# Attention results moved by transfers within SBUF, denominators on eight rows, gate by exponential, a first lead of 20 slots

## The chip, the cores and the metric

The kernel runs on one core of one Trainium2 chip. The metric is the device time of the whole kernel in microseconds, the median of several runs. All matrix work is TensorE's (PE), and DVE, ACT (ScalarE) and POOL (GpSimd) are the engines beside it; SP only issues transfers and waits.

## The reference

One layer of a transformer on x of 4 x 1024 x 128 in f32, cut to what matters:

```
a   = layernorm(layernorm(x)) * ln_g + ln_b           # the inner one is the block's, the outer the attention's
q, k, v = split(a @ w_qkv + b_qkv)                     # 16 heads of 8 dimensions
p   = softmax(q k^T / sqrt(8) + relative_bias)         # 1024 x 1024 for each of 4 x 16 heads
x   = x + layernorm((p v) @ w_out + b_out)
h   = layernorm(x)
s   = sigmoid(h @ gate^T);  sfc = s + e_bias           # 64 experts in 8 groups
eight experts of the four best groups by sfc; weights s / sum(s) * 2.5; capacity 128 per expert
y   = sum of weight * w2(silu(w1 h) * (w3 h))  +  a shared expert of the same form
out = x + layernorm(y)
```

## The kernel before

The 4096 tokens are 8 chunks of 512 (4 tiles of 128). The kernel has four parts, one behind the other.

*Projection (project_tokens).* For each chunk the tokens are normalised, transposed and multiplied by w_qkv. q and k are cut into three bf16 pieces each and stored to DRAM as q_image and k_image; v gets its bias by an addition on DVE (add_v, L291) and is stored as v_columns with a column of ones behind each head's eight, nine in all. DVE fills the fixed rows of the stacks at the very start (L296). The relative bias is a product of sines too: its query and key rows stand in bias_q_image and bias_k_image, and load_bias_side (L141) loads them into the stacks of four groups of four heads, group 0's on SP's queue here, those of groups 1 to 3 on ACT's queue at the start of the next part: 54 transfers.

*Attention and routing (attend_and_route).* There are 32 units: a batch, one half of its queries (512) and a group of four heads. Each engine has its own instruction stream, written out in steps; 32 steps make a unit. In a step TensorE makes a transposed score of 128 keys by 512 queries (scores_t, L1219) in one of three banks (st_bank), and ACT takes its exponential (L1141) into probs. The order in which users take the three banks is a list (ring_places): each place waits until the place three before it is free. In every second step TensorE makes one slot of row scores (row_scores, L1206) in one of two double banks, and DVE takes its maximum (row_max, L692); 16 slots make a unit, and they run LEAD = 26 slots ahead of the steps. When the maxima of a unit are complete, POOL splits the negative maximum in two bf16 pieces (split_shift), TensorE transposes it (turn_shift, L1242, at step J_MTURN = 18 of the unit before), ACT copies it (shift_copy, L1059), and SP puts it into the query stack with four transfers (put_shift, L636). The first step of the unit waits for them.

Every four steps TensorE multiplies the probabilities with the values (times_values, L1228): four heads side by side in four column tiles, 9 columns each, into one bank (pv_bank). The products stand after steps PV_AFTER = (9, 13, 16, 20, 24, 27, 31, 35). In the next unit ACT copies the bank to unit_out (out_copy, L1066, step 4), TensorE transposes it in four pieces (turn_out, L1237, step 8), and ACT copies the result to att (rows_copy, L1075): rows are tokens then, and the ninth column of each head is its denominator.

When four units have given 512 tokens of 16 heads, the chunk is routed while the next four units run: DVE takes reciprocals of 128x64 denominators (L719), POOL multiplies (normalise, L913), TensorE transposes (turn_att), ACT copies (copy_att), TensorE multiplies with w_o, and so on through two layer norms, the transposition of the result (L1264), the gate's logits, and ACT's Sigmoid (gate_scores, L1111). Sigmoid and Exp are in different activation tables. The selection of the experts goes to and fro between DVE and POOL. RING_AT, NORM_Y, RECIP and their like say in which unit of four and at which step each piece stands; NORMALISE, BIASED and their like do the same for POOL, in eighths of a unit. POOL writes each chunk's rows to the experts' table with 32 indirect transfers (scatter, L1002), one in each eighth of a unit; those of the last chunks run behind the last unit.

*SP's queue.* Before: loads of groups 1 to 3, the first shift, 12 constants, and then in each unit the next batch's loads of one group (13 transfers, 12 units have them), the next shift, and clearing of the tables.

*Experts (run_experts) and the last layer norm (finish)* follow. They are not touched.

Of the kernel before, what the change touches and what calls it, by code (L numbers as in the profile page):

```python
# [18 lines left out]
ALU = mybir.AluOpType  # L19
# [3 lines left out]
P = 128  # L23
# [11 lines left out]

VW = HD + 1
# [64 lines left out]
class Stacks:  # L101
# [3 lines left out]
    def __init__(self, ctx, nc):  # L105
# [4 lines left out]
        self.values = [sb(f"values{g}", [P, TILES_T, HG, VW]) for g in range(GROUPS)]  # L110
# [6 lines left out]
        self.vst = [sb(f"vst{a}", [P, PER, H, VW]) for a in range(2)]  # L117
# [15 lines left out]
def load_values(engine, stacks, v_columns, b, g):  # L133
    engine.dma_start(stacks.values[g][:].rearrange("p k h c -> p k (h c)"),
                     v_columns[:, b * TILES_T:(b + 1) * TILES_T, HG * VW * g:HG * VW * (g + 1)]).then_inc(stacks.loaded[g], 16)

# [4 lines left out]
def load_bias_side(engine, stacks, bias_q_image, bias_k_image, g, side):  # L141
    mine = slice(SIDE_HEADS * side, SIDE_HEADS * (side + 1))
    heads = slice(HG * g + SIDE_HEADS * side, HG * g + SIDE_HEADS * (side + 1))
    for r, places in Q_PLACED(side, bias=True):
        engine.dma_start(stacks.q[g][r:r + 2 * HD, :, mine, :].rearrange("r c h i -> r c (h i)"),
                         bias_q_image[:, places, :, heads, :].rearrange("c u e h i -> (u e) c (h i)")).then_inc(stacks.bias_rows_in[g], 16)
    for r, places in K_PLACED(side, bias=True):
        for c in range(2):
            engine.dma_start(stacks.k[g][r:r + 2 * HD, c, mine, :],
                             bias_k_image[c, places].rearrange("u e (o i) -> (u e) o i", o=1).to_broadcast([2 * HD, SIDE_HEADS, CHUNK])).then_inc(stacks.bias_rows_in[g], 16)  # L150


LOAD_BIAS = 16 * 9 * SIDES


def project_tokens(nc, x, ln_g, ln_b, w_qkv, b_qkv, w_rel_rows, q_table, k_table, ident_in, ident,
# [3 lines left out]
    with ExitStack() as ctx:  # L160
# [12 lines left out]
        bv = sb("bv", [P, DIM])  # L173
# [11 lines left out]
        half_made, ones_made, scaled_b = sem("half_made"), sem("ones_made"), sem("scaled_b")  # L185
# [8 lines left out]
        CONSTS, BIAS_CONSTS = 8 * 16, 3 * 16  # L194
# [3 lines left out]
        def _(sp):  # L198
# [4 lines left out]
            for dst, src in (  # L203
# [4 lines left out]
                (bv[:], b_qkv[2 * DIM:3 * DIM].rearrange("(o d) -> o d", o=1).to_broadcast([P, DIM])),  # L208
# [12 lines left out]
            for c in range(CHUNKS):  # L221
# [8 lines left out]
                sp.dma_start(v_columns[:, c * PER:(c + 1) * PER, :], vst[a][:].rearrange("p j h c -> p j (h c)")).then_inc(v_stored[a], 16)  # L230
# [8 lines left out]
                if c in (1, 2):  # L239
                    load_bias_side(sp, stacks, bias_q_image, bias_k_image, 0, c - 1)  # L240
# [11 lines left out]
        def _(dve):  # L252
# [33 lines left out]
            def add_v(c):  # L286
                a = c % 2
# [1415 lines left out]
```

## Time and the profile before

| | |
|---|---|
| median of 3 runs | 1190.63 us (1190.5 to 1190.64) |
| profiled execution | 1190.24 us, of which the span is 1188.4 us |
| mean granted clock | 0.882 |
| PE busy | 895.0 us (75%) |
| DVE busy | 782.7 us (66%) |
| ACT busy | 718.9 us (60%) |
| POOL busy | 579.1 us (49%) |
| first transposed score | 111.6 us |
| last copy out of the value bank | 903.9 us |
| first expert's rows loaded from the table | 1011.8 us |

The shares of busy time are means over stages with different limits, so they are read by stage. An engine's idle time is given with what ended it. A matmul's length in the timeline contains its way through the array; the distance between two starts is what it holds the engine. Some matmul records are missing.

### The profile page before, as it was taken

The numbers are of one execution on the slowest core, as the hardware profiler recorded it, in microseconds if no ns is written. First come the engines' busy times: TensorE is split into PE (matmuls) and PEld (weight loads), VectorE is DVE, ScalarE is ACT, GpSimd is POOL, SyncE is SP. The second block draws the span as 40 slices with busy tenths as digits, with TensorE's granted clock in tenths as the row PEclk, the third lists the DMA queues.
The fourth block names the chain that finished last, engine by engine and source line by source line (L and its number), as shares of the span: only waits on it lengthen the run. The fifth ranks groups of instructions, "written<-read, shape, count | busy, mean of one in ns | idle before, by whom it ended". The sixth has DMA issues, their size and how long they took to land. (4 is left out here: it accounts for less than half of the span.)

```text
span 1188.4 us, 16269 instructions
## 1 busy us (share of the span) xinstructions
PE 895.0 (75%) x5166; PEld 292.5 (25%) x5248; DVE 782.7 (66%) x1222; ACT 718.9 (60%) x1452; POOL 579.1 (49%) x724
## 2 busy tenths in 40 slices
PE   4545999999999999998999999999886450655400
PEld 2310222222222222222222222222222330443300
DVE  7977888779788888887987887897730320111107
ACT  4521777787787778778778877877885110322204
POOL 5621000112455454544644554463566775478847
PEclk9865999999999999999999999999998675656655
DMA  4798110122410022210001111000000010767546
GB/s 101 232 238 119 34 54 28 48 68 62 103 34 26 25 55 54 70 35 3 3 3 35 34 41 27 3 3 2 2 2 3 28 37 11 186 125 136 101 95 210
DMA packets 109292, 73.59 MB, mean 62 GB/s; under 512 B 39711, under 2 KB 94747, under 8 KB 109206
## 3 DMA queue, kind: packets, MB, share of 16 engines
q1 hardware_dynamic: 84470, 63.01, 19.7%
q0 software_dynamic: 21504, 6.79, 4.8%
q10 hardware_dynamic: 3232, 2.73, 1.6%
q8 instruction: 42, 0.69, 0.2%
q14 instruction: 44, 0.36, 0.1%
HBM read 39.99 MB, written 54.95 MB: 80 GB/s over the span
## 5 line engine op out<-in xcount | busy, mean ns | idle before, releaser
L692 DVE TENSOR_REDUCE half_max<-s_pair 128x2 f32<-128x1024 f32 x512 | 602.9, 1217 | 138.7 <-PE s_pair L1206 134.1
L1141 ACT ACTIVATE probs<-st_bank 128x512 f32<-128x512 f32 x1024 | 554.8, 602 | 173.8 <-PE st_bank L1219 147.5
L1002 POOL DMA_INDIRECT table<-rows,keys_i x256 | 255.5, 998 | 258.9 <-PE pv_bank L1228 120.1
L1219 PE MATMUL st_bank<-q_stack,k_stack 98*128 98x512 bf16 (+1 forms) x942 | 320.8, 387 | 35.2 <-ACT probs L1141 25.5
L1228 PE MATMUL pv_bank<-probs,values 128*9 128x512 f32 x2048 | 267.7, 595 | 1.9 <-issue 0.2
L1206 PE MATMUL s_pair<-k_stack,q_stack 64*128 64x512 bf16 x1024 | 205.7, 399 | 21.6 <-DVE half_max L692 19.8
L1219 PEld LDWEIGHTS st_bank<-q_stack,k_stack 98*128 98x128 bf16 (+1 forms) x1024 | 81.6, 97 | 252.1 <-ACT probs L1141 150.3
L1415 POOL DMA_INDIRECT sums<-out,ids x64 | 99.0, 1547 | 41.5 <-ACT out L1470 18.7
L1206 PEld LDWEIGHTS s_pair<-k_stack,q_stack 64*128 64x128 bf16 x1024 | 49.2, 93 | 275.6 <-issue 160.4
L1429 DVE CAST ids<-xe 128x4 uint32<-128x4 f32 x16 | 2.7, 168 | 131.6 <-DMA sums<-out,ids 84.8
L1506 PE MATMUL psY<-down_w,h 64*128 64x128 f32 x128 | 18.4, 434 | 46.4 <-DVE h L1442 46.4
L898 POOL CAST shift<-minus_max 128x16 bf16<-128x16 f32 x32 | 6.8, 212 | 94.9 <-DVE minus_max L699 93.9
L1470 ACT ACTIVATE out<-psY,w_cur 128x128 f32<-128x128 f32 x64 | 18.3, 368 | 55.8 <-PE psY L1506 55.2
L1483 PE MATMUL psX<-const_ident,xe 128*128 128x128 f32 x64 | 16.5, 407 | 45.8 <-DMA xe<-table 45.8
L1228 PEld LDWEIGHTS pv_bank<-probs,values 128*9 128x9 f32 x2048 | 30.3, 88 | 67.5 <-issue 39.9
L1603 ACT ACTIVATE whole<-whole,lessE,rstdE 128x128 f32<-128x128 f32 x32 | 13.2, 482 | 43.4 <-POOL lessE L1596 43.4
L1454 ACT COPY xeT<-psX 128x512 f32<-128x512 f32 x16 | 9.4, 585 | 40.2 <-PE psX L1483 33.6
L1495 PE MATMUL psH<-xeT,up_w 128*64 128x128 f32 x256 | 30.3, 413 | 2.3 <-issue 1.7
L1059 ACT CAST shiftT<-st_bank 32x128 bf16<-32x128 f32 x32 | 7.7, 240 | 32.7 <-issue 32.7
L1237 PE MATMUL st_bank<-const_ident,unit_out 128*128 128x128 f32 x128 | 20.1, 280 | 9.1 <-ACT probs L1141 8.2
L1506 PEld LDWEIGHTS psY<-down_w,h 64*128 64x128 f32 x128 | 13.9, 298 | 52.2 <-DVE h L1442 52.2
L1495 PEld LDWEIGHTS psH<-xeT,up_w 128*64 128x64 f32 x256 | 24.0, 214 | 5.9 <-issue 4.7
(181 smaller groups left out, 803.4 us busy)
## 6 DMA issues: line engine op xcount, KB each, us to landing
table<-blank SPq DMA_DIRECT2D x8, 772.0 KB, 4.8
xe<-table SPq DMA_DIRECT2D x16, 386.0 KB, 5.1
q_stack<-q_image SPq DMA_DIRECT2D x96, 64.0 KB
k_stack<-k_image SPq DMA_DIRECT2D x96, 64.0 KB
s<-sums SPq DMA_DIRECT2D x24, 256.0 KB, 6.1
k_image<-k_piece SPq DMA_DIRECT2D x16, 256.0 KB, 2.9
table<-rows,keys_i POOLq DMA_INDIRECT x256
sums<-zeros SPq DMA_DIRECT2D x16, 256.0 KB
```

The costliest lines, as they stand in the source:

```text
L692: V.tensor_reduce(half_max[n % 2][:, h:HG:SIDE_HEADS, tile, half], s_pair[slot % S_SLOTS][:].rearrange("p (s k) -> p s k", s=SIDES), AX.X, ...
L1002: pool.indirect_dma_start(out=table, out_offset=bass.IndirectOffsetOnAxis(ap=keys_i[c % 2][:, pick:pick + 1], axis=0), in_=rows[c % 2][:, ...
L1141: A.activation(probs[:, s % P_SLOTS, :], st_bank[at % ST_BANKS][:], ACT.Exp).then_inc(bank_free, 1)
L1206: mm = M(s_pair[slot % S_SLOTS][:, side * CHUNK:(side + 1) * CHUNK], q_stack[g][own, half, head, tile * P:(tile + 1) * P], k_stack[g][own, ...
L1219: M(bank(at)[:], k_stack[g][own, tile // PER, h, tile % PER * P:(tile % PER + 1) * P], q_stack[g][own, half, h, :], start=True, stop=True) ...
L1228: mm = M(pv_bank[PART * h:PART * h + VW, :], values[n % GROUPS][:, tile, h, :], probs[:, (s + h) % P_SLOTS, :], start=(tile == 0), stop=(t ...
L1237: mm = nc.tensor.transpose(to[:, t * P:(t + 1) * P], unit_out[:, t * P:(t + 1) * P], ident[:])
L1415: pool.indirect_dma_start(out=sums[n % SUMS], out_offset=bass.IndirectOffsetOnAxis(ap=ids[a][:, q:q + 1], axis=0), in_=out[a][:, q, :], in ...
L1470: A.activation(out[r % DEEP][:, q, :], psY[q % 2][:, q // 2 * P:(q // 2 + 1) * P], ACT.Copy, scale=w_cur[r % DEEP][:, q:q + 1]).then_inc(o ...
L1483: mm = nc.tensor.transpose(psX[a][:, q * P:(q + 1) * P], xe[r % DEEP][:, q, 0:DIM], ident[:])
L1495: mm = M(psH[a][half:half + F, m * P:(m + 1) * P], up_w[a][:, (which * Q + q) * F:(which * Q + q + 1) * F], xeT[a][:, q * P:(q + 1) * P], ...
L1506: mm = M(psY[q % 2][:, m * P:(m + 1) * P], h[a][half:half + F, m * P:(m + 1) * P], down_w[a][half:half + F, m * DIM:(m + 1) * DIM], start= ...
```

## The change

1. *Values.* The values are stored with 8 columns a head, without bias and without ones, sorted by dimension and then head. ACT copies them (copy_v). One tensor, values, holds for each tile 32 value columns and 32 ones that are filled once. A head's product takes every fourth column of the 64: 8 values and 8 ones, 16 columns for 9, so that its denominator comes out on eight rows.
2. *Moves.* Eight transfers on SP for each unit (move_out) put each head's eight result rows and eight denominator rows from unit_out to the partitions of its dimensions in sums_t and denominators: the chunk is then already transposed. turn_out, rows_copy, turn_att and copy_att are gone. The reciprocal is over 128x512 elements, POOL multiplies, and the result is projected.
3. *Bias of the values.* Since the probabilities sum to one, it is multiplied with w_o once (value_bias) and added to the output's bias (output_bias) in unit 2.
4. *Gate.* ACT takes exp(-x), POOL adds one, DVE takes the reciprocal of 128x256.
5. *Start.* SP loads group 1, then puts the first shift, then loads groups 2 and 3; the constants come behind the shift of unit 1. ACT loads the query rows of the bias from DRAM and copies the key rows from group 0's stack, 30 transfers for 54. 20 slots run ahead at first, and one more is added every eight steps up to 26. POOL's set-up follows the second shift.
6. *Places.* The value products stand after steps 7, 11, 15, 19, 23, 27, 31 and 35; most places of the routing move by 2 to 6 steps, and the scatters by an eighth of a unit.

```diff
-        self.values = [sb(f"values{g}", [P, TILES_T, HG, VW]) for g in range(GROUPS)]
+        self.values = sb("values", [P, GROUPS, TILES_T, 2, HD * HG])
...
+def copy_bias_keys(engine, stacks, g, side):
+    for r, rows in ((MAIN_AT[side] + MAIN_ROWS, MAIN_ROWS), (REST_AT[side] + REST_ROWS, REST_ROWS)):
+        engine.dma_start(side_of(stacks.k[g], r, rows, side), side_of(stacks.k[0], r, rows, side)).then_inc(stacks.bias_rows_in[g], 16)
...
-            def add_v(c):
...
-                V.tensor_tensor(vst[a][:, :, :, 0:HD], psV[a][:].rearrange("p (j h d) -> p j h d", j=PER, h=H),
-                                bv[:].rearrange("p (o h d) -> p o h d", o=1, h=H).to_broadcast([P, PER, H, HD]), ALU.add).then_inc(v_done, 1)
...
+            V.memset(stacks.values[:, :, :, 1, :].rearrange("p g k c -> p (g k) c"), 1.0).then_inc(stacks.gaps_done, 1)
...
+            def copy_v(c):
...
+                for j in range(PER):
+                    ins = A.copy(vst[a][:, :, j, :].rearrange("p g (d h) -> p g h d", h=HG), psV[a][:, j * P:(j + 1) * P].rearrange("p (g h d) -> p g h d", g=GROUPS, h=HG))
...
-PV_AFTER = (9, 13, 16, 20, 24, 27, 31, 35)
-J_UOUT, J_OTURN, J_MTURN = 4, 8, 18
+PV_AFTER = (7, 11, 15, 19, 23, 27, 31, 35)
+J_UOUT, J_BO = 4, 10
+BO_UNIT = 2
...
-RING_AT = {"att": (0, 17), "y": (0, 22), "xf": (1, 25), "logits": (1, 30), "ranks": (3, 2)}
-NORM_Y, NORM_XF = (1, 2), (1, 18)
-RECIP, STATS_Y, STATS_X1 = (0, 12), (0, 26), (1, 10)
-TOP1, COUNT, SECOND, GSUM, GRANK, BEST, MARK, WEIGHTS, KEYS = (2, 6), (2, 8), (2, 12), (2, 14), (2, 20), (2, 24), (2, 26), (3, 2), (3, 10)
+RING_AT = {"y": (0, 26), "xf": (1, 28), "logits": (1, 31), "ranks": (3, 4)}
+NORM_Y, NORM_XF = (1, 4), (1, 22)
+RECIP, STATS_Y, STATS_X1 = (0, 18), (0, 30), (1, 14)
+GATE, TOP1, COUNT, SECOND, GSUM, GRANK, BEST, MARK, WEIGHTS, KEYS = (2, 6), (2, 10), (2, 12), (2, 16), (2, 18), (2, 24), (2, 28), (2, 30), (3, 6), (3, 14)
...
-NORMALISE, OUT_NORM, RESIDUAL, RES_NORM = (0, 3), (0, 7), (1, 2), (1, 4)
-BIASED, TOPS, ORDER, KEEP, CHOOSE, SLOTS_AT = (2, 1), (2, 2), (2, 4), (2, 5), (2, 7), (3, 1)
-SPLIT, SCATTER = 3, 3 * TILES_T + 3
+NORMALISE, OUT_NORM, RESIDUAL, RES_NORM = (0, 5), (0, 7), (1, 2), (1, 5)
+GATE_ONE, BIASED, TOPS, ORDER, KEEP, CHOOSE, SLOTS_AT = (2, 0), (2, 2), (2, 3), (2, 5), (2, 6), (3, 0), (3, 2)
+SPLIT, SCATTER = 3, 3 * TILES_T + 4
...
+def MTURN(n):
+    return 22 if n == 0 else 18
...
+def issued(step):
+    return min(ALL_UNITS * SLOTS, step // 2 + 1 + FIRST_LEAD + min(LEAD - FIRST_LEAD, step // 8))
...
+            def move_out(n):
+                c, g = n // GROUPS, n % GROUPS
+                sp.wait_ge(unit_out_done, n + 1)
+                if c >= 1 and g == 0:
+                    sp.wait_ge(normed_done, c)
+                for h in range(HG):
+                    to = slice((HG * g + h) * HD, (HG * g + h + 1) * HD)
+                    for v, dst in enumerate((sums_t, denominators)):
+                        sp.dma_start(dst[to, :], unit_out[PART * h + v * HD:PART * h + (v + 1) * HD, :]).then_inc(unit_moved, 16)
...
-                V.reciprocal(recip[:], att[c % 2][:, :, :, HD]).then_inc(recip_done, 1)
+                dve.wait_ge(unit_moved, MOVED * GROUPS * (c + 1))
+                V.reciprocal(denominators[:], denominators[:]).then_inc(recip_done, 1)
+            def gate_scores(c):
+                dve.wait_ge(plus_one_done, c + 1)
+                V.reciprocal(scores[:], scores[:]).then_inc(gate_done, 1)
...
+                G.tensor_tensor(att[:], sums_t[:], denominators[:], ALU.mult).then_inc(normed_done, 1)
...
+            act.wait_ge(bias_rows_in[0], LOAD_BIAS[0])
             for g in range(1, GROUPS):
                 for side in range(SIDES):
-                    load_bias_side(act, stacks, bias_q_image, bias_k_image, g, side)
+                    load_bias_queries(act, stacks, bias_q_image, g, side)
+                    copy_bias_keys(act, stacks, g, side)
...
-                    act.wait_ge(bank_ready, after(place["out", n - 1]))
+                    act.wait_ge(unit_moved, MOVED * n)
                 A.copy(unit_out[:], pv_bank[:]).then_inc(unit_out_done, 1)
...
-                A.activation(scores[:].rearrange("p t e -> p (t e)"), st_bank[at % ST_BANKS][:, 0:PER * E], ACT.Sigmoid).then_inc(bank_free, 1)
+                A.activation(scores[:].rearrange("p t e -> p (t e)"), st_bank[at % ST_BANKS][:, 0:PER * E], ACT.Exp, scale=-1.0).then_inc(bank_free, 1)
...
-                    mm = M(pv_bank[PART * h:PART * h + VW, :], values[n % GROUPS][:, tile, h, :],
+                    mm = M(pv_bank[PART * h:PART * h + 2 * HD, :],
+                           values[:, n % GROUPS, tile].rearrange("p u c -> p (u c)")[:, h:2 * HD * HG:HG],
                            probs[:, (s + h) % P_SLOTS, :], start=(tile == 0), stop=(tile == TILES_T - 1),
```

## Rows read from the trace of the kernel before

**Rows 1.** View of stages, two stretches: busy us, (instructions), clock, DMA share, GB/s.

```profile
200.00:300.00 100.00, 93.51 (x561) 25.20 (x569) 83.72 (x115) 78.26 (x155) 18.79 (x38) 1.00 0.22 60
...
900.00:1000.00 100.00, 42.40 (x163) 24.48 (x159) 20.32 (x63) 19.69 (x37) 72.98 (x87) 0.69 0.08 23
```

**Rows 2.** Timeline of a regular stretch, all engines: start us, length us, what, [idle before].

```profile
180.03 1.05 PE L1228 MATMUL pv_bank<-probs,values 128*9 128x512 f32 x8
...
181.01 0.39 PE L1206 MATMUL s_pair<-k_stack,q_stack 64*128 64x512 bf16 x2
...
181.33 0.60 PE L1219 MATMUL st_bank<-q_stack,k_stack 98*128 98x512 bf16 x2
...
181.44 2.36 DVE L692 TENSOR_REDUCE half_max<-s_pair 128x2 f32<-128x1024 f32 x2 [0.34 <-PE s_pair L1206]
...
181.75 1.57 ACT L1141 ACTIVATE probs<-st_bank 128x512 f32<-128x512 f32 x3 [0.64 <-PE st_bank L1219]
...
182.73 1.05 PE L1228 MATMUL pv_bank<-probs,values 128*9 128x512 f32 x8
```

**Rows 3.** Timeline of PE, where other work comes in.

```profile
163.34 0.63 PE L1237 MATMUL st_bank<-const_ident,unit_out 128*128 128x128 f32 x4 [0.19 <-ACT probs L1141]
...
171.24 0.23 PE L1242 MATMUL st_bank<-ident,shift 128*32 128x128 bf16 x1 [0.25 <-issue]
...
258.46 0.39 PE L1219 MATMUL st_bank<-q_stack,k_stack 128*128 128x512 bf16 x1 [1.53 <-ACT probs L1141]
...
258.78 0.62 PE L1228 MATMUL pv_bank<-probs,values 128*9 128x512 f32 x4
```

**Rows 4.** Timeline of ACT, copies out of the value bank, one per unit.

```profile
184.95 0.58 ACT L1066 COPY unit_out<-pv_bank 128x512 f32<-128x512 f32 x1
...
208.27 0.58 ACT L1066 COPY unit_out<-pv_bank 128x512 f32<-128x512 f32 x1
...
233.44 0.59 ACT L1066 COPY unit_out<-pv_bank 128x512 f32<-128x512 f32 x1
...
261.00 0.58 ACT L1066 COPY unit_out<-pv_bank 128x512 f32<-128x512 f32 x1
...
308.52 0.58 ACT L1066 COPY unit_out<-pv_bank 128x512 f32<-128x512 f32 x1
```

**Rows 5.** Timeline of the start of the attention, several engines.

```profile
94.57 0.29 PE L1242 MATMUL st_bank<-ident,shift 128*32 128x128 bf16 x1 [2.43 <-POOL shift L900]
...
101.61 0.25 ACT L1059 CAST shiftT<-st_bank 32x128 bf16<-32x128 f32 x1 [32.74 <-issue]
...
101.89 2.87 SPq L636 DMA_DIRECT2D q_stack<-shiftT  x4
...
111.62 1.03 PE L1219 MATMUL st_bank<-q_stack,k_stack 98*128 98x512 bf16 x2 [5.16 <-DMA q_stack<-shiftT]
```

**Rows 6.** View of DMA issues: count, KB each, median us to landing.

```profile
k_stack<-bias_k_image SPq DMA_DIRECT2D x12, 32.0 KB, 2.0
```

**Rows 7.** Groups of instructions: count, busy us, mean ns, idle before.

```profile
L1228 PEld LDWEIGHTS pv_bank<-probs,values 128*9 128x9 f32 x2048 | 30.3, 88 | 67.5 <-issue 39.9 <-ACT probs L1141 17.4 <-ACT shiftT L1059 5.7
...
L719 DVE RECIPROCAL recip<-att 128x64 f32<-128x64 f32 x8 | 4.4, 544 | 16.0 <-ACT att L1075 16.0
...
L785 DVE RECIPROCAL wrec<-wsum 128x4 f32<-128x4 f32 x8 | 1.4, 178 | 0.3
...
L1111 ACT ACT_TABLE_LOAD x7 | 9.0, 1283 | 0.1
```

**Rows 8.** Timeline of SP, one load's issue.

```profile
237.91 0.43 SPq L134 DMA_DIRECT2D values<-v_columns  x1
```

**Rows 9.** Timeline of DVE and POOL behind the last unit.

```profile
905.49 0.55 DVE L719 RECIPROCAL recip<-att 128x64 f32<-128x64 f32 x1 [15.99 <-ACT att L1075]
...
933.41 0.97 POOL L1002 DMA_INDIRECT table<-rows,keys_i  x1 [0.30 <-issue]
...
934.40 0.74 POOL L949 TENSOR_TENSOR sfc<-scores,const_e_bias 128x256 f32<-128x256 f32 x1
```

More of the change, by code:

```diff
@@ L345, in _ @@
             inverse(0)
-            for a in range(2):
-                G.memset(vst[a][:, :, :, HD:VW], 1.0).then_inc(ones_made, 1)
             inverse(1)
@@ L502, in ring_places @@
                 order.append(("step", n * STEPS + j))
-            if j == J_OTURN and 1 <= n <= ALL_UNITS:
-                order.append(("out", n - 1))
-            if j == J_MTURN and n < ALL_UNITS - 1:
+            if n < ALL_UNITS - 1 and j == MTURN(n):
                 order.append(("shift", n + 1))
+            if (n, j) == (BO_UNIT, J_BO):
+                order.append(("bo", 0))
             if n >= GROUPS:
@@ L664, in _ @@
                 if n == 0:
+                    for dst, src in later:
+                        sp.dma_start(dst, src, allow_slow_non_contiguous=True).then_inc(later_in, 16)
                     sp.wait_ge(zeros_done, 1)
@@ L807, in shared_h @@
                 V.tensor_tensor(s_h[c % 2], s_pair[c % 2][:, CHUNK:2 * CHUNK], s_h[c % 2], ALU.mult).then_inc(s_h_done, 1)
[L809 removed]
+            for slot in range(FIRST_LEAD):
                 row_max(slot)
@@ L1021, in _ @@
                         residual_norm(c)
+                    elif now and at == GATE_ONE:
+                        gate_plus_one(c)
                     elif now and at == BIASED:
@@ L1231, in times_values, with value_bias @@
                 mm.then_inc(pv_done, 1)
-            def turn_out(n):
-                pe.wait_ge(unit_out_done, n + 1)
-                to = bank(place["out", n])
-                for t in range(PER):
-                    mm = nc.tensor.transpose(to[:, t * P:(t + 1) * P], unit_out[:, t * P:(t + 1) * P], ident[:])
-                mm.then_inc(bank_ready, 1)
+            def value_bias():
+                pe.wait_ge(setup_done, SETUP)
+                M(bank(place["bo", 0])[0:3, 0:DIM], bv3[:], k["w_o"][:], start=True, stop=True).then_inc(bank_ready, 1)
             def turn_shift(n):
@@ L1243, in turn_shift, with project @@
                   start=True, stop=True).then_inc(bank_ready, 1)
-            def turn_att(c):
+            def project(c):
                 pe.wait_ge(normed_done, c + 1)
-                to = bank(place["att", c])
-                for t in range(PER):
-                    mm = nc.tensor.transpose(to[:, t * P:(t + 1) * P], normed[:, t, :], ident[:])
-                mm.then_inc(bank_ready, 1)
-            def project(c):
-                pe.wait_ge(bank_free, after(place["att", c]))
                 to = bank(place["y", c])
```

187 lines of the change are left out of this document (93 added, 94 removed).

## The prediction

> **What bounds the kernel now.** I read the table by stage first. From 200 to 300 us, in the middle of the attention, TensorE is busy 93.5 of 100 us at full clock, DVE 84, ACT 78, POOL 19 [rows 1]. After the attention TensorE has 42 and POOL 73 [rows 1]: the end of the routing hangs on POOL's scatters. So there are three stages, each with its own limit.
>
> The timeline of a regular stretch shows how TensorE is bound. Four steps make one pattern: a value product, two row scores, four transposed scores. It starts at 180.03 and again at 182.73: 2.70 us [rows 2]. The value product holds 0.98 (180.03 to 181.01), a row score 0.32, a pair of transposed scores 0.54 (181.33 to 181.87). ACT waits 0.64 for TensorE and DVE 0.34 in each pattern. A single transposed score costs 0.32 (258.46 to 258.78) [rows 3], so a pair that something splits costs 0.10 more.
>
> The starts of the copies out of the value bank give the length of a unit: 23.32 us where there is no routing (184.95 to 208.27); with routing four units take 100.25 (208.27 to 308.52), 6.97 more than 4 x 23.32, and the second of them alone 27.56 (233.44 to 261.00) [rows 4]. Eight patterns are 21.60, so 1.72 us of each plain unit is no pattern.
>
> The start of the attention is a chain of its own: the shift's transpose is done by 94.9, but ACT copies it only at 101.61, after 32.74 us of issuing the bias transfers, SP issues it at 101.89, and the first transposed score runs at 111.62 because it waits for that transfer [rows 5]: 16.7 us.
>
> **The change, part by part.** The sum is made against the profiled execution, 1190.24 us (span 1188.4), 0.39 below the median of 1190.63.
>
> *Head.* A fill of 1,024 elements is added ahead of DVE's first statistics; DVE needs 1.18 us for a reduction over as many [rows 2]. One addition per chunk leaves DVE for four small ACT copies, which fit ACT's gap in each chunk. Bounds -0.5 and +1.2; I take **+0.2**.
>
> *Start.* ACT issues 30 bias transfers for 54, some 14 us, and is free before the shift is ready. SP loads group 1 only before the shift. So copy at about 95.3, four issues in 2.87 [rows 5] to 98.3. Landing: at least 2.0, as for the early bias key transfers [rows 6], at most the 6.9 from the last issue (about 104.7) to 111.6 seen under load [rows 5]. Fewer bytes are queued ahead, so I take 3.5, near the low end: first score at 101.8. **-9.8** (bounds -11.3 and -6.4). Groups 2 and 3 load afterwards and are wanted some 15 us later.
>
> *Plain part of the units.* Removed: the four transposes of a unit's result with their waits (0.63 and 0.19 of it [rows 3]), ACT's second copy, and three value products that split a pair; the bank ring has one place less. In the new order every product stands after an odd step. What stays besides eight patterns is the shift's transpose between the two steps of a pair: 0.16 + 0.10 = 0.26 [rows 3]. A unit is then 21.86, 1.46 less. ACT's copy of the bank, 0.58 [rows 4], fits its 0.64. 29 units at 1.46, 0.3 for unit 0 (it has no transposes), 0.8 each for the last two, which have few row scores and lie nearer ACT's pace: 42.3 + 0.3 + 1.6 = **-44.2**.
>
> *Slots moved.* Six slots that ran while TensorE waited now run inside units 0 and 1: 6 x 0.32 = 1.9. There five row scores come in eight steps: 5 x 1.18 = 5.9 on DVE against 2 x 2.70 + 0.32 = 5.72 on TensorE, so DVE just binds; 1.0 for that. **+2.9** (1.9 to 5).
>
> *Wider weights.* The value products load 16 columns for 9, four elements apart. The trace has no such form. If nothing scales it costs 0. If what the product holds beyond four streams (0.98 - 0.86 = 0.12; a stream is half of 0.54, less overlap) grows by 16/9, it is 0.09. I take 0.02, near the low end: a load takes 88 ns [rows 7], so eight of them already lie under the streams but for 0.12. 256 products: **+5.1** (0 to 23).
>
> *Routed groups, seven in the attention.* The reciprocal changes from 128x64 to 128x512 elements. Rows: 4 elements 178 ns, a 128x64 one 544 ns [rows 7]: 5.8 ns per element on top of 0.17. Hence 3.2 us for 512, and 1.7 for the gate's 256. DVE has only two score buffers, so the lead of 26 slots doesn't help. I lay it on the pattern: after the second row maximum (2.64 into it) DVE is away until 5.8, the next two maxima end at 6.95 and 8.1; the row score due at 5.40 needs the first, the one due at 6.26 + 1.55 the second: 1.55 + 0.3 = 1.85 lost. The gate's costs 0.35. Gone are two table loads per group (1.28 each [rows 7]), which stall TensorE 1.53 [rows 3], the transposes of the chunk (0.6), and a stall of 0.6 at the residual's statistics. But ranks, normalising and the copy no longer fall where ACT was late anyway: 1.0. Broken pairs 0.2. Sum per group 1.85 + 0.35 + 1.0 + 0.2 - 1.53 - 0.6 - 0.6 = +0.7; with a split at the ranks I take 0.9: 7 x 0.9 = **+6.3** (0 to 17).
>
> The Trainium skill (VectorE: DVE Perf Modes, "First, the fixed hardware budget") says that a reciprocal runs an iterative divide with a repeat count of 8. By that the rows' 5.8 ns per element would be 8 cycles, and the sum would be that of rival 2; the row of 64 elements speaks against it.
>
> *The moves.* Eight transfers of 16 KB on SP for each unit, behind nothing but in front of the next batch's 13 loads (0.43 each [rows 8], 5.6 us) and of the next shift. At 0.43 to 0.72 each [rows 5, 8] and 2.0 to land [rows 6] they are there 5.4 to 7.8 us after the copy. The copy ends 1.75 us after the product at step 3 does; the reciprocal follows the row maximum of step 18, three patterns and 2.64 after that product, 10.7: 9.0 us after the copy. In units with loads the next shift goes out 1.75 + 3.4 (to 5.8) + 5.6 = 11 to 13 us into the seven patterns, 18.9, that end where it is needed, and takes 2.9 + 2.0. Hidden: 0.
>
> *Moved set-up.* SP's constants, POOL's set-up and, in unit 2, the output bias (one product, one ACT copy, ten POOL passes) come later, but are wanted from unit 4 on, and POOL has 19 of 100 us of work in units 4 to 7, where routing has begun [rows 1], and less before: 0. The first shift's transpose of unit 1 goes from step 18 to 22; three patterns, 8.1 us, remain for 2.9 + 2.0: 0.
>
> *Tail.* After the last unit nothing hides it. The moves take 5.7 for 1.0 of transposes and copy, the reciprocal 3.2 for 0.5 [rows 7, 9]; saved are the chunk's transposes and copy, 1.3. That is 6.1. POOL then has one more scatter before the last chunk's keys, 0.97 + 0.30 [rows 9], and one pass of about 0.75 (such an addition at 934.40 [rows 9]), and waits some 0.8 for the exponential. **+8.9** (7 to 12).
>
> Sum: 0.2 - 9.8 - 44.2 + 2.9 + 5.1 + 6.3 + 8.9 = -30.6. 1190.24 - 30.6 + 0.39 = **1160.0 us**.
>
> **Rivals.**
> 1. *The weight loads show.* For it: four column tiles are loaded before each product and the columns are strided. Against: a load of 88 ns [rows 7] for 9 columns is mostly not columns, or eight would not fit. At 0.09 a product 18 us more than the sum: 1178. The Trainium skill (TensorE: Matmul & The Clock Gate, "LDWEIGHTS (loading the stationary operand)") lets a load grow with its columns, 1/1.2 ns each; that would be 47 ns for eight loads, all exposed.
> 2. *The long reciprocals cost a third more.* If an element takes eight of the steps of which a plain one takes about one (1.18 us for 1,024), 4.8 us and 2.5: 1.6 and 0.8 more, so 2.4 on each of seven groups and 1.6 in the tail: 18 more, 1178. For it: DVE is then busy over nine tenths of a group. Against: the two rows of the same operation. This is the skill's repeat count as a mechanism.
> 3. *The moves come late, slower than before.* If the last lands after the reciprocal's turn, DVE stands, then TensorE one for one, in seven groups, and once more in the tail. From 9.0 + 30.6/8 = 12.8 us after the copy it is slower than before. The worst rows together [rows 5], 8 x 0.72 + 6.9 = 12.7, give 8 x 3.7 = 30 more: 1190; at 14 us 1200. For it: the transfers have eight partitions each. Against: the queues' share is 0.22 from 200 to 300 us [rows 1].
> 4. *The start isn't gained*, as the copied bias keys load the queues just so: 6 to 8 lost, 1167.
> 5. *Less friction*: landing in 2.0, weights at 0, groups at 0: 1160 - 1.5 - 5 - 6 = 1148.
>
> **Chances.** The forecast (1153 to 1168) 0.52; rival 1 0.10; rival 2 0.12; rival 3 0.10, half of it slower than before; rival 4 0.08; rival 5 0.08. The range from 1150 to 1177 leaves out rival 3, much of rival 5 and half of 1 and 2. Faster than before by over 0.2%, about what a measurement of this kernel can tell, 0.92; within it 0.03; slower 0.05.
>
> **What would show it.** The first transposed score near 102; plain units of 21.9 to 22.0 between copies of the value bank; a pattern of 2.70 to 2.72 (rival 1: 2.79); the reciprocal at 3.2 us and one idle stretch of TensorE of 1.5 behind it; no table load between the first exponential and the tail; the end of the attention to the first expert some 9 us longer. The prediction is wrong if DVE waits for the moves, if a product holds over 1.05, or if another wait takes the place of the transposes, as for the value bank's copy.

## The result

The changed kernel takes **1183.83 us** (median of 4 runs, 1181.16 to 1185.66); the kernel before takes 1190.64 in the same comparison. The ratio is 0.994, 95% interval 0.9919 to 0.9961: 0.6% faster. Forecast were 1160.0, range 1150 to 1177. The direction was right and the size was not: of 30.6 us of gain 6.8 came. The profiled execution is the slowest of the four, 1185.66 with a span of 1183.8.

View of stages of the changed kernel, the stretches of [rows 1]: busy us, (instructions), granted clock, DMA share, GB/s.

```profile
200.00:300.00 100.00, 95.29 (x570) 24.86 (x564) 90.56 (x119) 75.33 (x153) 23.00 (x42) 1.00 0.25 68
...
900.00:1000.00 100.00, 30.85 (x118) 19.27 (x116) 20.21 (x55) 17.83 (x30) 68.57 (x81) 0.65 0.08 23
```

In the middle of the attention TensorE is busy 95.3 for 93.5 and DVE 90.6 for 83.7. The engine that had room before the change has little left.

The copies out of the value bank, timeline of ACT, answer to [rows 4]. The first two rows bound a plain unit, the third and fourth end the first two units of a routed group; the fence below it has the first unit of a later group.

```profile
179.34 0.58 ACT L1128 COPY unit_out<-pv_bank 128x512 f32<-128x512 f32 x1
...
201.84 0.58 ACT L1128 COPY unit_out<-pv_bank 128x512 f32<-128x512 f32 x1
...
227.25 0.58 ACT L1128 COPY unit_out<-pv_bank 128x512 f32<-128x512 f32 x1
...
252.25 0.58 ACT L1128 COPY unit_out<-pv_bank 128x512 f32<-128x512 f32 x1
```
```profile
691.55 0.58 ACT L1128 COPY unit_out<-pv_bank 128x512 f32<-128x512 f32 x1
...
718.51 0.58 ACT L1128 COPY unit_out<-pv_bank 128x512 f32<-128x512 f32 x1
```

A plain unit takes 22.50 (179.34 to 201.84), for 23.32 before and 22.02 forecast (21.86 and eight products at 0.02 more). A group's first unit takes 25.41 (201.84 to 227.25), but 26.96 at 691.55. Four units with routing take 97.03 (400.54 to 497.57, a group without a clock fall; the first group takes 97.41), for 100.25 before and 95.95 forecast.

The start, timelines of several engines, answers to [rows 5]:

```profile
96.66 0.29 PE L1291 MATMUL st_bank<-ident,shift 128*32 128x128 bf16 x1 [2.43 <-POOL shift L954]
...
96.99 0.25 ACT L1121 CAST shiftT<-st_bank 32x128 bf16<-32x128 f32 x1 [25.53 <-PE st_bank L1291]
...
97.27 2.89 SPq L666 DMA_DIRECT2D q_stack<-shiftT  x4
...
101.17 0.61 PE L1257 MATMUL s_pair<-k_stack,q_stack 64*128 64x512 bf16 x2 [0.62 <-DVE half_max L737]
...
101.72 1.04 PE L1270 MATMUL st_bank<-q_stack,k_stack 98*128 98x512 bf16 x2
```

The transpose comes 2.1 later than before (96.66 for 94.57), ACT takes it at once, and the first transposed score runs at 101.72. The prediction said 101.8. TensorE doesn't wait for the transfer any more: up to the first transposed score it makes the row scores of the 20 slots, and what it waits for between them is DVE's maxima (0.62 ahead of the last pair).

**Where the gain went.** Both profiled executions are laid along the same marks; "forecast" is made of the prediction's terms.

| stretch | before | after | change | forecast | missed by |
|---|---|---|---|---|---|
| start to first transposed score | 111.62 | 101.72 | -9.9 | -9.6 | -0.3 |
| to the copy that ends unit 1 | 50.00 | 54.64 | +4.6 | +1.4 | 3.2 |
| units 2 to 31 | 742.23 | 726.03 | -16.2 | -31.4 | 15.2 |
| last copy to first expert load | 107.94 | 122.47 | +14.5 | +8.9 | 5.6 |
| experts and finish | 176.6 | 178.9 | +2.3 | 0 | 2.3 |

The marks before are 111.62, 161.62, 903.85 and 1011.79, after 101.72, 156.36, 882.39 and 1004.86. The last column adds up to 26.0, more than the 23.8 between the medians, because the profiled execution is the slowest. Six tenths of the miss lie in units 2 to 31. Three things in the trace can make it up.

*One: two short waits in every unit.* Timelines of PE and ACT around the copy and around the shift's transpose, in a plain stretch:

```profile
188.01 0.23 PE L1291 MATMUL st_bank<-ident,shift 128*32 128x128 bf16 x1
...
188.40 0.39 PE L1270 MATMUL st_bank<-q_stack,k_stack 128*128 128x512 bf16 x1 [0.16 <-ACT probs L1194]
...
191.44 1.07 PE L1279 MATMUL pv_bank<-probs,values 128*16 128x512 f32 x8
```
```profile
201.34 0.60 ACT L1194 ACTIVATE probs<-st_bank 128x512 f32<-128x512 f32 x1 [0.66 <-PE st_bank L1270]
...
201.84 0.58 ACT L1128 COPY unit_out<-pv_bank 128x512 f32<-128x512 f32 x1
...
202.30 1.60 ACT L1194 ACTIVATE probs<-st_bank 128x512 f32<-128x512 f32 x3
...
202.56 1.06 PE L1279 MATMUL pv_bank<-probs,values 128*16 128x512 f32 x8 [0.18 <-ACT unit_out L1128]
...
205.28 1.07 PE L1279 MATMUL pv_bank<-probs,values 128*16 128x512 f32 x8
```

The pattern is 2.72 (202.56 to 205.28), as forecast with 0.02 for the wider weights. But the transposed score behind the shift's transpose waits 0.16 for ACT, and the product at 202.56 waits 0.18 for the copy, which ACT begins only behind the exponential of step 4. With 0.26 for the transpose a unit should hold 8 x 2.72 + 0.26 = 22.02. The other 0.48 stands at these two places.

*Two: the long reciprocal,* timelines of DVE and PE in an ordinary group, and groups of instructions with count, busy us and mean ns:

```profile
410.40 3.34 DVE L762 RECIPROCAL denominators<-denominators 128x512 f32<-128x512 f32 x1
```
```profile
414.88 0.39 PE L1257 MATMUL s_pair<-k_stack,q_stack 64*128 64x512 bf16 x2 [1.19 <-DVE half_max L737]
...
416.01 0.39 PE L1257 MATMUL s_pair<-k_stack,q_stack 64*128 64x512 bf16 x2 [0.20 <-DVE half_max L737]
...
416.97 1.16 PE L1299 MATMUL st_bank<-const_w_o,att 128*128 128x128 f32 x8
...
418.27 1.07 PE L1279 MATMUL pv_bank<-probs,values 128*16 128x512 f32 x8
```
```profile
L1279 PEld LDWEIGHTS pv_bank<-probs,values 128*16 128x16 f32 x2048 | 41.5, 115 | 69.4 <-issue 64.7 <-ACT probs L1194 4.7
...
L762 DVE RECIPROCAL denominators<-denominators 128x512 f32<-128x512 f32 x8 | 26.7, 3344 | 19.9 <-DMA denominators<-unit_out 19.9
```

DVE is away for 3.34, and TensorE waits 1.19 and 0.20 for it: 1.39, where the prediction had 1.85. All 19.9 us of idle time ahead of the reciprocals lie behind the last unit; inside the attention the moves were always in time. What the Trainium skill states (VectorE: DVE Perf Modes, "First, the fixed hardware budget": a repeat count of 8 for the reciprocal) can be held against these rows: from 64 elements [rows 7] to 512 it is (3344 - 544) / 448 = 6.25 ns per element, 5.4 times the 1.15 of a plain reduction (1.18 us for 1,024). The trace stays below eight times, which would be 9.2 ns (the prediction put its 5.8 there, by mistake), and rival 2 fell with it.

*Three: TensorE's clock,* timeline of PE in the unit of 26.96, at the place that the rows above show for an ordinary one:

```profile
705.90 0.39 PE L1257 MATMUL s_pair<-k_stack,q_stack 64*128 64x512 bf16 x2 [1.19 <-DVE half_max L737]
...
707.02 0.39 PE L1257 MATMUL s_pair<-k_stack,q_stack 64*128 64x512 bf16 x2 [0.20 <-DVE half_max L737]
...
708.01 2.08 PE L1299 MATMUL st_bank<-const_w_o,att 128*128 128x128 f32 x8
...
709.88 0.63 PE L1270 MATMUL st_bank<-q_stack,k_stack 128*128 128x512 bf16 x1
...
710.44 1.46 PE L1279 MATMUL pv_bank<-probs,values 128*16 128x512 f32 x8
```

The wait for DVE is the same 1.19 and 0.20. But then the projection takes 2.08 where it took 1.16, and the product 1.46 for 1.07. The granted clock over this unit is 0.94, and in these 3 us it is at the lower of its two levels, 1.2 GHz for 2.4. It cost 1.55. The same is seen in the units that end at 328.97 and 817.10, and in no unit of the kernel before behind its first. It was not in the prediction at all.

*In the tail,* timelines of DVE and POOL behind the last unit:

```profile
950.61 0.69 DVE L852 TENSOR_TENSOR probs<-s_pair,probs 128x512 f32<-128x512 f32 x1 [2.13 <-ACT probs L1179]
...
954.16 0.69 DVE L852 TENSOR_TENSOR probs<-s_pair,probs 128x512 f32<-128x512 f32 x1 [2.13 <-ACT probs L1179]
...
956.12 0.18 DVE L846 TENSOR_SCALAR keys_i<-keys 128x32 uint32<-128x32 f32 x1
```
```profile
957.09 0.98 POOL L1057 DMA_INDIRECT table<-rows,keys_i  x1 [8.33 <-DVE keys_i L846]
```

POOL stands 8.33 us for the last chunk's slot keys, and DVE makes them at 956.12, behind eight products for the shared expert (two for each of its last four chunks). The keys went from step 10 to step 14 of that unit, and those products stand at step 12. The prediction had looked at what the keys' move does to POOL's queue and not at what they pass in DVE's own.

### The profile page after: what moved, and what is told of

It is laid out like the page before. It is cut to its first block and busy times, and to the rows that moved or that the text cites. A ratio compares the mean times of both kernels' runs of the same rounds, so it can differ in the third digit from the quotient of the medians.

```text
span 1183.8 us, 16193 instructions
## 1 busy us (share of the span) xinstructions
PE 888.7 (75%) x5090; PEld 285.7 (24%) x5090; DVE 808.8 (68%) x1223; ACT 692.4 (58%) x1433; POOL 591.1 (50%) x732
## 5 line engine op out<-in xcount | busy, mean ns | idle before, releaser
L1194 ACT ACTIVATE probs<-st_bank 128x512 f32<-128x512 f32 x1024 | 543.9, 603 | 184.7 <-PE st_bank L1270 163.8
L1270 PE MATMUL st_bank<-q_stack,k_stack 98*128 98x512 bf16 (+1 forms) x1024 | 326.0, 388 | 15.4 <-issue 8.4
L1279 PE MATMUL pv_bank<-probs,values 128*16 128x512 f32 x2048 | 274.9, 608 | 4.3 <-ACT unit_out L1128 4.2
L1270 PEld LDWEIGHTS st_bank<-q_stack,k_stack 98*128 98x128 bf16 (+1 forms) x1024 | 78.9, 97 | 177.3 <-issue 95.8
L1279 PEld LDWEIGHTS pv_bank<-probs,values 128*16 128x16 f32 x2048 | 41.5, 115 | 69.4 <-issue 64.7
L762 DVE RECIPROCAL denominators<-denominators 128x512 f32<-128x512 f32 x8 | 26.7, 3344 | 19.9 <-DMA denominators<-unit_out 19.9
L967 POOL TENSOR_TENSOR att<-sums_t,denominators 128x512 f32<-128x512 f32 x8 | 10.1, 1257 | 39.7 <-DVE denominators L762 39.7
L1600 DVE TENSOR_TENSOR whole<-s 128x512 f32<-128x512 f32 x8 | 5.4, 678 | 31.0 <-DMA s<-sums 31.0
```

The lines of the kernel that those rows point to most:

```text
L762: V.reciprocal(denominators[:], denominators[:]).then_inc(recip_done, 1)
L1194: A.activation(probs[:, s % P_SLOTS, :], st_bank[at % ST_BANKS][:], ACT.Exp).then_inc(bank_free, 1)
L1270: M(bank(at)[:], k_stack[g][own, tile // PER, h, tile % PER * P:(tile % PER + 1) * P], q_stack[g][own, half, h, :], start=True, stop=True) ...
L1279: mm = M(pv_bank[PART * h:PART * h + 2 * HD, :], values[:, n % GROUPS, tile].rearrange("p u c -> p (u c)")[:, h:2 * HD * HG:HG], probs[:, ...
```

## The experiments

The kernel before took 1190.8 in the company of the first four runs (15 runs), 1184.77 (one run) beside the next four, and 1184.89 (9 runs) beside the last three. So each time is compared with the kernel before beside which it ran, and the length of units decides wherever it can: a plain unit repeats to 0.02 us from run to run.

**Keys ahead of the shared products.**

```diff
-SHARED_PE, SHARED_ACT, SHARED_DVE = ((1, 0), (2, 0), (3, 4)), ((1, 8), (2, 0), (3, 4)), ((1, 12), (2, 16), (2, 22), (3, 12))
+SHARED_PE, SHARED_ACT, SHARED_DVE = ((1, 0), (2, 0), (3, 4)), ((1, 8), (2, 0), (3, 4)), ((1, 12), (2, 16), (2, 22), (3, 16))
```

> The last chunk's slot keys stand ahead of the shared expert's last four products in the vector engine's queue (those move from step 12 to step 16 of the last routing unit). Theory, the late keys are a term of the tail that the sum lacked: POOL's wait of 8.3 us for the keys goes, the tail from the last bank copy to the first expert load shrinks from 122.5 to about 115, time 1175 to 1177. Rival, the wait only uncovers the next one (the stores of the shared expert's results or the scatters' own pace): 1182 to 1184.

1178.75 us, ratio 0.9899 (0.987 to 0.9927). Timeline of its POOL, behind the last unit:

```profile
946.62 0.99 POOL L1057 DMA_INDIRECT table<-rows,keys_i  x1 [0.30 <-issue]
...
947.91 0.98 POOL L1057 DMA_INDIRECT table<-rows,keys_i  x1 [0.30 <-issue]
...
983.07 0.98 POOL L1057 DMA_INDIRECT table<-rows,keys_i  x1 [2.05 <-issue]
...
985.59 0.98 POOL L1057 DMA_INDIRECT table<-rows,keys_i  x1 [1.54 <-issue]
```

The wait of 8.33 is gone. Two others of 2.05 and 1.54 have come, for nothing that the profile names; the kernel before has two such (1.62 and 1.83) near the same place. The tail is 117.5 for 122.5. So both expectations had a part of the truth: the keys cost 5.0 of the 5.6 us that the tail missed.

**The reciprocal in pieces, and the reciprocal cut down.** The first kernel makes the reciprocal in four pieces, at steps 16, 18, 20 and 22 for the one at 18, and the gate's in two. The second leaves out 448 of the 512 elements.

```diff
-                V.reciprocal(denominators[:], denominators[:]).then_inc(recip_done, 1)
+                part = denominators[:, t * P:(t + 1) * P]
+                V.reciprocal(part, part).then_inc(recip_done, 1)
...
-                    if now == RECIP:
-                        sum_reciprocals(c)
+                    if now[0] == RECIP[0] and 0 <= j - RECIP[1] < 2 * PER:
+                        sum_reciprocals(c, (j - RECIP[1]) // 2)
```

> The 512-element reciprocal of the denominators is cut into four of 128 at steps 16, 18, 20 and 22, and the gate's 256 into two at steps 6 and 8; the same elements are computed. Theory A, the single long absence of the vector engine stalls TensorE by 1.4 us in each of seven groups and brings about the clock falls in three of them (7.5 us together): both go, 1167 to 1173. Theory B, the falls have another cause: 1.4 to 1.0 us less in each group alone, 1174 to 1177. Rival, the vector engine has no slack to take up the pieces, so the loss is only spread: 1182 to 1185.

```diff
-                V.reciprocal(denominators[:], denominators[:]).then_inc(recip_done, 1)
+                V.reciprocal(denominators[:, 0:E], denominators[:, 0:E]).then_inc(recip_done, 1)
```

> Leaves work out: of the denominators only the first 64 columns are inverted, the other 448 are used as they are. This prices the long reciprocal. By its duration 2.8 us less vector work in each of eight groups. Theory A (it also brings about the clock falls): 7 x 1.2 + 7.5 + 2.8 in the tail = 19 less, 1163 to 1167. Theory B (the falls have another cause): 11 less, 1171 to 1174. Rival, the reciprocal costs TensorE nothing that something else does not take: only the tail's 2.8, 1181.

The pieces made it slower than the kernel before: 1198.28, ratio 1.0066 (1.0045 to 1.0087). None of the three expectations had that. Timeline of PE and POOL in one of its groups:

```profile
419.70 0.39 PE L1259 MATMUL s_pair<-k_stack,q_stack 64*128 64x512 bf16 x2 [0.66 <-DVE half_max L737]
...
420.59 1.26 POOL L969 TENSOR_TENSOR att<-sums_t,denominators 128x512 f32<-128x512 f32 x1 [6.53 <-DVE denominators L763]
...
421.90 0.39 PE L1299 MATMUL st_bank<-bo_rows,ones 3*128 3x512 bf16 x1 [1.49 <-POOL att L969]
...
422.22 2.08 PE L1301 MATMUL st_bank<-const_w_o,att 128*128 128x128 f32 x8
```

For the row maxima behind the pieces TensorE waits only 0.66 where it waited 1.39. But the last piece ends at 420.5, the multiplication on POOL follows until 421.85, and the projection, which stands at step 26 in TensorE's order, waits 1.49 for it. And now the clock falls in every one of the seven groups (0.84 to 0.94 over their first unit), which then takes 27.7 to 31.5 for 25.4.

With 64 elements it is 1165.36, ratio 0.9796 (0.9765 to 0.9827), as theory A said. The same row of ACT as above, a group's first unit:

```profile
395.55 0.58 ACT L1128 COPY unit_out<-pv_bank 128x512 f32<-128x512 f32 x1
...
419.44 0.58 ACT L1128 COPY unit_out<-pv_bank 128x512 f32<-128x512 f32 x1
```

23.89 for 25.41: the 448 elements cost 1.52 in each of seven groups, 10.6 us. Over no unit of this run behind the first is the granted clock below 1.00. By itself that could be luck: the eight profiled executions with the whole reciprocal at step 18 have a fall in 15 of 56 groups. But the four without its stall (this one, the last run below, the kernel before, and that kernel with the exponential) have none in 28. So the falls hang on the stall that the reciprocal makes, though not on its length alone. The kernel before waits 1.53 for ACT at its table loads [rows 3], and this kernel stands 1.18 and 1.00 within 3.5 us in one unit, both without a fall. What else decides is not shown.

**The lead.**

```diff
-LEAD, FIRST_LEAD = 26, 20
+LEAD, FIRST_LEAD = 26, 26
```

> The lead is 26 slots from the start, as before the change, so the six slots are run ahead of unit 0 again and not inside units 0 and 1. Theory, the six slots cost 3.3 us more than forecast inside the units, where four or five row scores in eight steps make the vector engine the bound, while ahead of unit 0 they cost 1.2 us each at the vector engine's pace less the 1 to 2 us of waiting that is left for the shift's transfer: first transposed score 5 to 6 us later, units 0 and 1 together 5 to 6 us shorter, time within 1 us of the change, 1183 to 1185. If the early slots were free under the transfer, as one may read before the change: 5 less, 1179. If they are not made up for: 5 more, 1189.

1185.69, ratio 0.9958 (0.9936 to 0.998), beside 0.994: no difference that can be told. The second copy out of the value bank comes at 157.48 for 156.36, with a unit 1 of 22.49 for 23.98. With 26 the first transposed score comes at 108.81 for 101.72, and units 0 and 1 then take 26.18 and 22.49 for 30.66 and 23.98. So six slots cost 7.1 ahead of unit 0 and 6.0 inside the units, 1.0 each, where the prediction gave them 2.9: that is 3.1 of the 3.2 missed there. The lower number of slots at first gains 1.1 us. The 7.1 also show what bounds the start now: with the transfer issued at nearly the same time (97.58 for 97.27), each slot more puts the first transposed score off by 1.1 to 1.2.

**Weights of nine columns.**

```diff
-                M(pv_bank[PART * h:PART * h + 2 * HD, :],
+                M(pv_bank[PART * h:PART * h + HD + 1, :],
-                       values[:, n % GROUPS, tile].rearrange("p u c -> p (u c)")[:, h:2 * HD * HG:HG],
+                       values[:, n % GROUPS, tile].rearrange("p u c -> p (u c)")[:, h:(HD + 1) * HG:HG],
```

> Leaves work out: the value products load 9 columns and write 9 rows again (still four elements apart), and the rows moved as denominators are the rows of sums. This prices the wider weights. Theory, 0.02 us a product: pattern of four steps 2.70 for 2.72, plain unit 22.3 for 22.50, weight load record back from 115 to about 90 ns, 5 us less in all. Rival, the stride or the tile of 16 rows costs more than the loads' length: the pattern falls below 2.68, or not at all (then the 0.02 is of something else).

This kernel leaves out the denominators: it moves rows of sums in their place. One run, 1176.68 beside 1184.77. A plain unit is 22.40 for 22.50, 0.0125 a product, and a routed group is shorter by some 0.27. Over 32 units that is some 2.3 us, where the prediction had 5.1. The last unit is 17.82 for 18.85, but it is 17.90 in a run below with all 16 columns, so that is not the width's. The pattern had risen by 0.02 with the change; the columns are 0.0125 of it, and whether the stride is the rest is not shown. (The record of one load is 88 ns long in the kernel before, 99 here and 115 in the changed kernel.) Rival 1, at 0.09 a product, is out.

**The transpose behind the pair, and the copy behind step 3.**

```diff
-    return 22 if n == 0 else 18
+    return 23 if n == 0 else 19
```

> The shift's transpose stands behind the odd step 19 (23 in unit 0), ahead of the value product, and splits no pair of transposed scores. Theory, the 0.41 us that it costs a plain unit (0.16 of its own, 0.10 for the broken pair, 0.16 of waiting for ACT) falls to 0.16: plain unit 22.25 for 22.50, 6 to 8 us in all, 1176. Rival, the transpose then delays the product and ACT's copy of it delays the exponentials behind the pair: 22.4 to 22.6, 1182 to 1186.

```diff
-J_UOUT, J_BO = 4, 10
+J_UOUT, J_BO = 3, 10
```

> ACT copies the value bank behind the exponential of step 3 and not of step 4. Theory, ACT stands idle for 0.66 just there and the copy is over 0.4 us earlier, so the next unit's first product no longer waits 0.18 for it and the row score behind it is not late: plain unit 22.25 to 22.3, 6 us in all. Rival, the exponential of step 4 comes 0.3 to 0.4 later and the transposed scores of step 7 wait for their bank: 22.5 or more.

One run each: 1176.7 and 1169.08 beside 1184.77, 0.7% and 1.3% below it, where the changed kernel was 0.6% below. Single times hold different numbers of clock falls (three and one), so the units decide: plain units of 22.27 and 22.25 for 22.50. Both theories were right to 0.05 there. In the second run, timeline of ACT and PE at the copy:

```profile
177.40 0.59 ACT L1128 COPY unit_out<-pv_bank 128x512 f32<-128x512 f32 x1
```
```profile
178.98 1.07 PE L1279 MATMUL pv_bank<-probs,values 128*16 128x512 f32 x8
...
181.70 1.07 PE L1279 MATMUL pv_bank<-probs,values 128*16 128x512 f32 x8
```

The copy ends a microsecond ahead of the product at 178.98, nothing waits, and the next product follows at 2.72.

**The table loads by themselves, in the kernel before.**

```diff
-                A.activation(scores[:].rearrange("p t e -> p (t e)"), st_bank[at % ST_BANKS][:, 0:PER * E], ACT.Sigmoid).then_inc(bank_free, 1)
+                A.activation(scores[:].rearrange("p t e -> p (t e)"), st_bank[at % ST_BANKS][:, 0:PER * E], ACT.Exp, scale=-1.0).then_inc(bank_free, 1)
```

> The kernel before with one edit: the gate's activation is the exponential of the negated logits, and the addition of one and the reciprocal are left out (the gate is then another function). This prices the two table loads of a routed group by themselves. Theory: 1.53 of TensorE's stall in each of seven groups and two table loads less in the tail: 100.25 falls to 98.6 for four units, the unit of 27.57 to 26.0, 10 to 14 us in all, 1177 to 1180. Rival, the loads lie where ACT was late anyway: under 5 us, 1186 to 1190.

One run, 1176.16 beside 1184.77. Timeline of its ACT:

```profile
233.46 0.59 ACT L1066 COPY unit_out<-pv_bank 128x512 f32<-128x512 f32 x1
...
259.65 0.58 ACT L1066 COPY unit_out<-pv_bank 128x512 f32<-128x512 f32 x1
```

The unit is 26.19 for 27.56 [rows 4]: 1.38 in each of seven groups, where the prediction credited 1.53. The table loads by themselves are worth 9.7 us in the attention; this kernel leaves out the addition of one and the gate's reciprocal, and what those take back no run prices. The reciprocal that the same change made eight times as long takes 10.6 back, before any fall of the clock.

**The fill at the head.**

```diff
-            V.memset(stacks.values[:, :, :, 1, :].rearrange("p g k c -> p (g k) c"), 1.0).then_inc(stacks.gaps_done, 1)
             norm_stats(0)
...
             norm_shift(1)
+            V.memset(stacks.values[:, :, :, 1, :].rearrange("p g k c -> p (g k) c"), 1.0).then_inc(stacks.gaps_done, 1)
```

> The changed kernel with the fill of ones (1,024 elements) moved in the vector engine's queue from ahead of the first statistics to behind the second chunk's. Theory, that fill is the head stage's 2.1 us (the attention begins at 76.3 for 74.2): the stage ends 1 to 2 us earlier. Rival, the four small copies of the values on ACT in each chunk set it: it ends within 0.3 of the changed kernel's.

The attention begins at 76.30 for 76.98, and at 74.89 before the change. TensorE's last products of the head stage are back at 65.85, as before the change, and the stage still ends 1.4 later. So a third of the 2.1 is the fill, and two thirds lie behind the last products. The values' copies, the rival, are not seen to hold it up there: ACT's last k_full starts 1.0 later (68.59 for 67.61) after a longer wait for a store (2.71 for 1.62), and the last copies come behind it, at 69.74. What makes the store late was not tried by itself.

**The three orders together, and the pieces with a later projection.**

> The changed kernel with three orders put right: the keys ahead of the shared expert's last products, the shift's transpose behind the pair (step 19), the copy out of the value bank behind step 3. If the gains add up: plain unit 22.02 (eight patterns of 2.72 and 0.26), which is what the prediction gave a plain unit, 0.48 us in 32 units = 15, and 5 for the keys: 1163 to 1166, 0.977 to 0.980 of before. Rival, the transpose and the copy hide in the same idle time of ACT and do not add up: plain unit 22.2, 1168 to 1172.

```diff
-RING_AT = {"y": (0, 26), "xf": (1, 28), "logits": (1, 31), "ranks": (3, 4)}
-NORM_Y, NORM_XF = (1, 4), (1, 22)
-RECIP, STATS_Y, STATS_X1 = (0, 18), (0, 30), (1, 14)
+RING_AT = {"y": (0, 28), "xf": (1, 28), "logits": (1, 31), "ranks": (3, 4)}
+NORM_Y, NORM_XF = (1, 6), (1, 22)
+RECIP, STATS_Y, STATS_X1 = (0, 16), (1, 0), (1, 16)
```

> As the kernel with three places, and the reciprocal in four pieces again (steps 16 to 22), with the projection at step 28 for 26 and the statistics behind it at step 0 of the next unit, so that TensorE does not wait 1.49 for the last piece. Theory, that wait and not the pieces made the run of the pieces slow and brought about its clock falls: the first unit of a group falls from 25.2 to 24.3 to 24.7, no clock falls, 5 to 8 us less than with the three places alone. Rival, four pieces cost the vector engine 3.75 for 3.34 and the row scores pay for it wherever the projection stands: the same time or up to 5 more.

| kernel | us | ratio to before | 95% interval |
|---|---|---|---|
| three orders | 1159.54 | 0.9777 | 0.9761 to 0.9793 |
| and pieces, projection at 28 | 1155.67 | 0.9752 | 0.9738 to 0.9766 |

Copies out of the value bank, ACT of the first:

```profile
176.73 0.58 ACT L1128 COPY unit_out<-pv_bank 128x512 f32<-128x512 f32 x1
...
198.75 0.58 ACT L1128 COPY unit_out<-pv_bank 128x512 f32<-128x512 f32 x1
```

The plain unit is 22.02, to the hundredth what the prediction gave it. In the second, timelines of DVE, POOL and PE in a group:

```profile
404.18 0.94 DVE L763 RECIPROCAL denominators<-denominators 128x128 f32<-128x128 f32 x1
...
405.20 1.27 POOL L968 TENSOR_TENSOR att<-sums_t,denominators 128x512 f32<-128x512 f32 x1 [6.52 <-DVE denominators L763]
...
406.89 0.39 PE L1298 MATMUL st_bank<-bo_rows,ones 3*128 3x512 bf16 x1
...
407.21 1.16 PE L1300 MATMUL st_bank<-const_w_o,att 128*128 128x128 f32 x8
```

The projection no longer waits (406.89 follows the score at 406.57), holds 1.16 at full clock, and no first unit of a group loses clock (one does in the run of the three orders). That unit falls from 25.17 to 24.45, the one behind it rises from 24.28 to 24.63, and the tail is 117.2 for 114.5. So of 5 to 8 us expected 3.9 came: the theory on the cause held, and the price in the tail was not in it.

## Why the prediction was wrong

**Bounds and start: right.** TensorE bounds the attention and POOL the tail. The start came at 101.72 for 101.8, though by luck: the head stage costs 2.1 for 0.2, and the shift's transfers land at most 1.6 after their last issue (97.27 + 2.89 to 101.72), where 3.5 was taken. The step behind it was wrong too: what holds TensorE until 101.72 is the row scores of the 20 slots at DVE's pace, not the transfer. Rival 4 is out.

**Plain units: the largest miss.** The removal of the transposes and the pattern of 2.72 were right. The failed step is "ACT's copy of the bank, 0.58, fits its 0.64", and with it the 0.26 for the shift's transpose. Idle time of ACT in a pattern is not idle time at the moment when the copy is due: ACT's 0.64 lies ahead of step 4's exponential, and the copy stood behind it. The copy's place cost 0.25 a unit and the transpose's 0.23 (the two single experiments), together 0.48 (the run with both). Over units 2 to 29 that is 13.4 of the 15.2 missed there; the last two units bring 2.4.

**Routed groups: the mechanism right, a little dear.** Without the 4 x 0.48, a group costs 95.1 for 95.95. The reciprocal took 3.34 for 3.2 (its two rows differ by 366 ns over 60 elements, 6.1 each, and the prediction used 5.8) and its stall 1.39 for 1.85; the table loads gave 1.38 for 1.53. That is 5.9 us better in seven groups.

**The clock: missing.** The reciprocal's stall was priced at its own length and no more. In three of seven groups of the profiled execution the granted clock then fell to its lower level for some 3 us, 1.55 to 1.6 each, 4.8 in all. In the runs here with the whole reciprocal at step 18 it is seen in one to three groups each; with 64 elements, with the pieces and the later projection, and in the kernel before, with Sigmoid or with the exponential, in none. (Near the end of the attention, where few row scores are left, the last three runs show 0.92 over one unit too; there the reciprocal has no part.) That it accounts for the spread of the changed kernel's runs, 4.5 us for 0.8 of the kernel before beside it, is not shown: the kernel with 64 elements spreads over 4.2 in four runs, and the kernel before over 5.1 in the nine beside the last three. The four entries, 13.4, 2.4, 4.8 and -5.9, leave 0.5 of the 15.2. In the unit from 299 to 329, TensorE stands twice for nothing named, 1.14 and 0.86, a little longer than the kernel before loses there (27.12 for 25.17). The kernel with 64 elements has these two as well (1.18 and 1.00). Why is open.

**Moved set-up: 0.5 for 0.** Unit 2 takes 22.98 for unit 3's 22.50, and so it does in every run of the changed kernel; the kernel before has 23.33 and 23.32. The product for the output's bias, timeline of PE, splits a pair there:

```profile
159.59 0.38 PE L1287 MATMUL st_bank<-const_w_o,bv 128*3 128x128 f32 x2
```

The pattern around it, 157.09 to 160.30, takes 3.21 for 2.72.

**Slots moved: 3.1 too little.** The term had 1.0 for DVE as the bound; by the run of the first lead units 0 and 1 paid 4.1. **Wider weights:** some 2.3 for 5.1. **Moves:** hidden, as said; 251 of the 256 issues take 0.62 to 0.66, below the 0.72 that was their upper bound, and five take 1.22 to 1.56. Rival 3 is out. **Tail:** up to the biased scores it cost 9.4 for 8.9; the keys behind the shared products, 5.0, were overlooked. **Experts:** 2.3 longer in this pair, but between 176.6 and 180.2 in the runs here whatever the edit; no cause was found.

With its steps at the right places (the three orders) the change has the plain unit of 22.02 that the prediction gave it. The whole gain isn't reached even so: 0.9777 of the kernel before, where 1160.0 is 0.9743 of 1190.63. That the run's 1159.54 us is so near 1160.0 means nothing, since the kernel before took 1184.89 beside it.

## What to carry to other kernels

Idle time of an engine within a repeated pattern is only worth something at the moment when the moved instruction may run: look up in the trace what stands ahead of it in the queue, and when its input is there, before a copy is called hidden. When a step moves by a few places in one engine's written order, list what it passes on that same engine; here four places put the keys behind eight products and cost 5 us. And where an engine with two buffers of lead is sent away for longer, cut the absence into pieces and move its consumer back by as much; pieces alone shift the wait to the consumer.

## What was not expected of the hardware

Behind a wait of TensorE of only 1.39 us (1.19 and 0.20) the granted clock can be down at 1.2 GHz for some 3 us: projection 2.08 for 1.16, product 1.46 for 1.07. It came in some groups and not in others with the same timeline to 0.02 us before it. The length of the wait doesn't tell it: the kernel before waits 1.53 at once [rows 3] and keeps its clock. With a wait of 1.49 close behind one of 0.66, in the run of the pieces, it came in all seven (in one of them the wait is 1.06 alone). Small transfers within SBUF, 16 KB each, take SP 0.62 to 0.66 apiece to issue (all but five of 256), and a fill of 1,024 elements takes DVE 0.91.
